# Transposing x and the context by VectorE blocks and a DRAM regroup in place of TensorE, in a self- and cross-attention kernel

## The reference

```python
def _attn(x, ctx, Wq, Wk, Wv, Wo, bo):
    q, k, v = x @ Wq, ctx @ Wk, ctx @ Wv        # 16 heads of 64
    sim = einsum('bihd,bjhd->bhij', q, k) * 64 ** -0.5
    return einsum('bhij,bjhd->bihd', softmax(sim), v) @ Wo + bo
h = _ln(x, g1, be1); x = _attn(h, h, ...) + x
h = _ln(x, g2, be2); x = _attn(h, context, ...) + x
h = _ln(x, g3, be3); y = h @ Wp + bp
x = a * gelu(gate) @ W2 + b2 + x                # a, gate: the halves of y
```

## Time and profile before

| what | value |
|---|---|
| median of 3 runs | 3034.53 us |
| the profiled execution | 3032.93 us, its span 3031.1 us |
| granted TensorE clock over the span | 0.995 |
| PE busy | 2969.6 us (98%) |
| PEld busy | 2591.1 us (85%) |
| DVE busy | 2296.2 us (76%) |
| ACT busy | 1883.4 us (62%) |
| POOL busy | 1424.5 us (47%) |
| DMA traffic | 625.06 MB, mean 206 GB/s |

### The profile page before, as it was taken

The page is one execution under the profiler, slowest core; times in us unless marked ns, Lnnn a source line. Parts: engine busy times, 40 slices in busy tenths (PEclk is TensorE's granted clock), DMA queues, the critical chain, the costliest instruction groups (busy, mean ns, idle before and its releaser), DMA issues. The chain is left out here.

```text
span 3031.1 us, 77419 instructions
## 1 busy us (share of the span) xinstructions
PE 2969.6 (98%) x25600; PEld 2591.1 (85%) x25600; DVE 2296.2 (76%) x3843; ACT 1883.4 (62%) x5618; POOL 1424.5 (47%) x976
## 2 busy tenths in 40 slices
PE   7999999999999999999999999999999979999999
PEld 6888888888888888788888888888888858888888
DVE  6777777777777777788888888888888855566554
ACT  6666666666666667677777777777777633223322
POOL 4555555555555555555555555555555530011000
PEclk9999999999999999999999999999999989999999
DMA  8788888888888888888888888888888830011000
GB/s 240 227 245 244 242 244 248 244 242 245 243 244 244 244 244 239 256 259 255 253 253 254 255 253 252 253 253 253 255 253 252 249 110 28 32 33 33 28 28 21
DMA packets 464444, 625.06 MB, mean 206 GB/s; under 512 B 57745, under 2 KB 397073, under 8 KB 464145
## 3 DMA queue, kind: packets, MB, share of 16 engines
q1 hardware_dynamic: 463024, 624.23, 69.1%
q10 hardware_dynamic: 1376, 0.27, 0.1%
HBM read 330.71 MB, written 293.60 MB: 206 GB/s over the span
## 5 line engine op out<-in xcount | busy, mean ns | idle before, releaser
L586 POOL TENSOR_TENSOR at_probs<-at_probs,at_row_inv 128x1024 f32<-128x1024 f32 x512 | 970.7, 1896 | 1057.8 <-DVE at_row_inv L792 1053.5
L637 ACT ACTIVATE at_probs<-at_ps_s,at_neg_max 128x256 f32<-128x256 f32 x2048 | 948.2, 474 | 143.0 <-DVE at_neg_max L765 94.3
L765 DVE TENSOR_REDUCE at_neg_max<-at_ps_s 128x2 f32<-128x512 f32 x1024 | 660.1, 683 | 193.6 <-PE at_ps_s L943 190.3
L784 DVE STREAM_TRANSPOSE at_blocks<-at_probs 128x1024 f32<-128x1024 f32 x512 | 630.9, 1232 | 2.7 <-POOL at_probs L586 2.0
L690 ACT ACTIVATE at_qk_hi<-at_ps_qk 128x512 fp32r<-128x512 f32 x512 | 305.9, 598 | 322.6 <-PE at_ps_s L943 182.5
L962 PE MATMUL at_ps_o<-at_probs_t,at_v 128*64 128x256 f32 x4096 | 500.3, 386 | 2.0 <-DMA at_probs_t<-at_turns 1.9
L875 PE MATMUL at_ps_qk<-at_h_hi,w_hi 128*128 128x256 f32 x1536 | 431.9, 304 | 11.3 <-ACT at_h_hi L660 4.9
L637 ACT ACTIVATION_READ_ACCUMULATOR at_probs<-at_ps_s,at_neg_max 128x1 f32 x2048 | 416.5, 203 | 0.0
L962 PEld LDWEIGHTS at_ps_o<-at_probs_t,at_v 128*64 128x64 f32 x4096 | 271.8, 137 | 148.9 <-issue 4.0
L875 PE MATMUL at_ps_qk<-at_h_hi,w_lo 128*128 128x256 f32 x1536 | 397.4, 281 | 0.0
L875 PEld LDWEIGHTS at_ps_qk<-at_h_hi,w_hi 128*128 128x128 f32 x1536 | 290.2, 189 | 123.0 <-issue 103.8
(11 more groups left out here) (108 smaller groups left out, 6617.3 us busy)
## 6 DMA issues: line engine op xcount, KB each, us to landing
at_turns<-at_blocks SPq DMA_DIRECT2D x2048, 128.0 KB, 2.5
at_probs_t<-at_turns SPq DMA_DIRECT2D x512, 512.0 KB, 4.4
at_xt<-in_x SPq DMA_DIRECT2D x32, 256.0 KB, 5.4
at_xres<-in_x SPq DMA_DIRECT2D x32, 256.0 KB, 3.3
after_self_attention<-at_yout SPq DMA_DIRECT2D x32, 256.0 KB, 2.6
at_xt<-after_self_attention SPq DMA_DIRECT2D x32, 256.0 KB, 5.6
at_xres<-after_self_attention SPq DMA_DIRECT2D x32, 256.0 KB, 3.6
after_cross_attention<-at_yout SPq DMA_DIRECT2D x32, 256.0 KB, 2.5
```

The source lines that it names most:

```text
L586: pool.tensor_tensor(tile, tile, scale, ALU.mult).then_inc(probs_ready, 1)
L637: last = act.activation(probs[:, slot % 2, h, t], scores[:, slot % 2, h, t], ACT.Exp, bias=neg_max[:, slot % 2, i:i + 1], accum_out=row_su ...
L765: nc.vector.tensor_reduce(neg_max[:, slot, r], scores[:, slot, h], AX_X, ALU.max, negate=True).then_inc(neg_max_ready, 1)
L784: nc.vector.transpose(blocks[:, slot].rearrange("p (j a q) -> p a j q", j=QUADS, q=QUAD), probs[:, slot].rearrange("p h t (k j q) -> p (h ...
```

## The change

For all sequences but the first of the program, the four TensorE transposes of x, the four of the context, and DVE's copy of the context out of the bank go. In their place DVE transposes 32x32 blocks of the normalised x (`turn_x`, at p = 4) and of the context (`turn_context`, at p = 2) into `x_blocks`, one buffer for both; SP stores them in four DMAs of 64 KB each to a DRAM buffer (`store_x`, `store_context`, after the probabilities' stores of that step) and loads them back with one DMA of 256 KB a step later (`load_x_back`, after the probabilities' loads of p = 6; `load_context_back`, after those of p = 4). `scale_shift` moves from step p = 4 to p = 6 on ACT, in front of `high_h`, and reads the loaded buffer `x_back`. The hi part of the context is made by two ACT instructions in place of one, since the source is now in another order. POOL normalises x in place, and one wait for the attention's last stores is added at the start of POOL's feed-forward work.

```diff
             def load_next(b, stage):
-                sp.wait_ge(xnorm_ready, b)
+                if isinstance(b, int) and b == 1:
+                    sp.wait_ge(h_transposed, 1)
+                else:
+                    sp.wait_ge(x_turned, b - 1)
                 sp.dma_start(xt[:], rows(x_in[stage][local])).then_inc(x_loaded, 16)
...
+            def store_bands(buffer, bands, stored):
+                for i in range(QUADS):
+                    sp.dma_start(bands[:, :, i].rearrange("j k n -> k j n"),
+                                 buffer[QUAD * i:QUAD * (i + 1)].rearrange("k (j n) -> k j n", j=QUADS)
+                                 ).then_inc(stored, 16)
+
+            def store_x(b):
+                sp.wait_ge(x_turned, b)
+                store_bands(x_blocks, x_turns, x_turn_stored)
...
+            def load_x_back(b):
+                sp.wait_ge(x_turn_stored, 16 * QUADS * b)
+                sp.dma_start(x_back[:], x_turns.rearrange("j k i n -> (j k) (i n)")).then_inc(x_back_loaded, 16)
...
+                if context and p == TURN_CONTEXT + 2:
+                    load_context_back(b + 1 - n)
+                if ahead(part, stage) and p == TURN_X + 2:
+                    load_x_back(b + 1)
                 for pair in (p, p + 1):
                     if alive(part, pair, TURNED):
                         store_turn(b, pair)
+                if context and p == TURN_CONTEXT:
+                    store_context(b + 1 - n)
+                if ahead(part, stage) and p == TURN_X:
+                    store_x(b + 1)
...
             def scale_shift(b, stage):
-                act.wait_ge(h_transposed, b + 1)
-                if counts(c := b):
-                    act.wait_ge(h_ready, c)
+                first = isinstance(b, int) and b == 0
+                if first:
+                    act.wait_ge(h_transposed, 1)
+                else:
+                    act.wait_ge(x_back_loaded, 16 * b)
+                    act.wait_ge(h_ready, b)
...
             def high_context(b):
-                act.wait_ge(c_t_ready, b - n + 1)
+                act.wait_ge(c_back_loaded, 16 * (b - n + 1))
...
-                act.activation(c_hi[:], c_t[:], ACT.Copy).then_inc(c_hi_ready, 1)
+                for k in range(KT):
+                    last = act.activation(tokens(c_hi[:, k]), by_token(c_t[:])[:, k], ACT.Copy)
+                last.then_inc(c_hi_ready, 1)
...
-                    if ahead(part, stage) and p == TURN_H:
+                    if ahead(part, stage) and p == 6:
                         scale_shift(b + 1, stage_ahead(part, stage))
-                    if ahead(part, stage) and p == 6:
                         high_h(b + 1)
...
-            def context_copy(local):
-                dve.wait_ge(c_transposed, local + 1)
-                nc.vector.tensor_copy(c_t[:].rearrange("p k q -> p (k q)"), ps_misc[:]).then_inc(c_t_ready, 1)
+            def turn_rows(rows, turned_rows):
+                nc.vector.transpose(x_blocks[:].rearrange("p (j a q) -> p a j q", j=QUADS, q=QUAD),
+                                    rows.rearrange("p t (k j q) -> p (t k) j q", j=QUADS, q=QUAD)
+                                    ).then_inc(turned_rows, 1)
...
+            def turn_x(b, stage):
+                dve.wait_ge(xnorm_ready, b + 1)
+                if stage == CROSS:
+                    dve.wait_ge(c_turn_stored, 16 * QUADS * (b - n + 1))
+                elif counts(c := 16 * QUADS * (b - 1)):
+                    dve.wait_ge(x_turn_stored, c)
+                turn_rows(xt[:], x_turned)
...
-                if ahead(part, stage) and p == TURN_CONTEXT and stage_ahead(part, stage) == CROSS:
-                    transpose_context(b + 1)
-                if ahead(part, stage) and p == TURN_H:
-                    transpose_h(b + 1, stage_ahead(part, stage))
```

More of the change, by code:

```diff
@@ L53 @@
 TURN = 2 * TT * TT * QUAD
-TURN_CONTEXT, TURN_H = 2, 4
+TURN_CONTEXT, TURN_X = 2, 4
+X_TURN = TT * KT * QUAD
 V_COLS = INNER // 4
@@ L458, in rows, with by_token, tokens @@
             return seq.rearrange("(t p) d -> p t d", p=P)
+        def by_token(buffer):
+            return buffer.rearrange("p (i t k q) -> p k t i q", i=QUADS, t=TT, k=KT)
+        def tokens(rows):
+            return rows.rearrange("p (t i q) -> p t i q", t=TT, i=QUADS)
         def stored_count(b, q):
@@ L510, in step @@
                         load_turn(b, pair)
+                context = ahead(part, stage) and stage_ahead(part, stage) == CROSS
                 if ahead(part, stage) and p == 0:
                     load_next(b + 1, stage_ahead(part, stage))
+                if context and p == TURN_CONTEXT + 2:
+                    load_context_back(b + 1 - n)
+                if ahead(part, stage) and p == TURN_X + 2:
+                    load_x_back(b + 1)
                 for pair in (p, p + 1):
@@ L642, in scale_shift @@
             def scale_shift(b, stage):
-                act.wait_ge(h_transposed, b + 1)
-                if counts(c := b):
-                    act.wait_ge(h_ready, c)
+                first = isinstance(b, int) and b == 0
[4 more added lines that the diff above has]
+                    act.wait_ge(h_ready, b)
                 for k in range(KT):
-                    last = act.activation(h_t[:, k], ps_misc[:, k * SEQ:(k + 1) * SEQ], ACT.Identity,
+                    out, source = ((h_t[:, k], ps_misc[:, k * SEQ:(k + 1) * SEQ]) if first else
+                                   (tokens(h_t[:, k]), by_token(x_back[:])[:, k]))
+                    last = act.activation(out, source, ACT.Identity,
                                           bias=beta_c[:, stage, k:k + 1],
@@ L814, in step @@
                     turn(b, p + 1)
+                if ahead(part, stage) and p == TURN_CONTEXT and stage_ahead(part, stage) == CROSS:
+                    turn_context(b + 1)
+                if ahead(part, stage) and p == TURN_X:
+                    turn_x(b + 1, stage_ahead(part, stage))
                 if alive(part, p + 1, NORMED):
@@ L881, in project_v @@
                     pe.wait_ge(v_ready, c)
-                if ahead(part, stage) and p == TURN_CONTEXT + 2 and stage_ahead(part, stage) == CROSS:
-                    pe.wait_ge(c_t_ready, b + 2 - n)
-                if ahead(part, stage) and p == TURN_H + 2:
-                    pe.wait_ge(h_t_ready, b + 2)
+                if part == FIRST and p == 0:
+                    pe.wait_ge(h_t_ready, 1)
                 if part in (FIRST, SEAM) and p == 0:
@@ L894, in project_v, with transpose_first @@
                 last.then_inc(v_done, 1)
-            def transposes(src, done):
+            def transpose_first():
+                pe.wait_ge(xnorm_ready, 1)
                 for k in range(KT):
@@ L1005, in _ @@
             pe.wait_ge(ident_made, 2)
[L1006 removed]
+            transpose_first()
             sequences(nc, pe, n, step)
@@ L1112, in _ @@
             pool.wait_ge(f.consts_loaded, 64)
+            pool.wait_ge(before, before_count)
             residual(0, 0)
```

57 lines of the change are left out of this document (30 added, 27 removed).

## The result

The changed kernel took 3133.1 us (median of 4, 3132.5 to 3133.7), the kernel before, beside it on the same chip, 3034.4 us. The ratio is 1.0328, its interval 1.0313 to 1.0343.

A forecast was written before the change was run, and what follows sets the result against it. PE was taken to bound both attention stages. From 3032.9 us, transposes removed gave -42.8, cross-attention stalls +55.7 and self-attention stalls +4.7: 3050.5, stated as 3051 us, range 3004 to 3104 us.

The forecast's parts named there:

- What bounds the kernel: Both attention stages: PE is busy without holes, so work taken off it is saved in full, 0.45 us a batch.
- DVE's turn and SP's stores: Each x and context: DVE's block transpose takes 0.6 us, hidden at p = 4; SP's four stores take 1.9 us.
- The chain behind s: From ACT's scale_shift: lo part of pair 7 ready at s + 3.85, packed lo part of the context at s + 4.91.
- The sum: Cross turn: PE waits for the context's packed lo part, 1.74 us in each of 32 sequences, 55.7 us in all.
- s, the landing of `x_back`: Cross-attention, p = 6: ACT starts scale_shift at s = 1979.4 (1977.8 to 1980.7), with x_back landing in 4.2 us.
- the two cases of the earlier trace: Landing of 256 KB before the change: median 5.5 us behind two 512 KB loads, 3.5 us with none in front.
- My second rival: Much slower: x_back lands in 5.5 us as DMA share rises towards 0.95; cross stall 3.04 us, 3106 us; chance 0.15.
- The probabilities' loads at nothing: Step p = 6: loads go out 1.9 us later but before their use, so cost nothing; at most 1.9 us.
- The stall in self-attention, 4.7 us: Lo part of pair 7 has 0.7 us left; scatter of landings costs 0.15 us for each of 31 sequences (0 to 19).

## Why the prediction was right or wrong

- **What bounds the kernel: right.** PE's time is saved in full wherever nothing else is late: self sequences are 0.45 us shorter, as predicted for a batch.
- **DVE's turn and SP's stores: right.** 0.67 us for 0.6 predicted (`at_x_blocks`, 667 to 671 ns in all 63), 1.83 us for 1.9.
- **The chain behind s: right, but for its last link.** The lo part of pair 7 was ready in time for PE to start at s + 3.78 (predicted s + 3.85); the packed lo part of the context took 0.42 us, as taken. The sum let this packed part decide; at this turn PE did not wait for it (done at 1963.28, read at 1963.63), and the wait for the lo part of pair 7 was the one that counted, 0.25 us less by the prediction's own figures. That PE would wait at the first `project_qk` of a cross sequence, and ACT for `x_back`, was also right.
- **s, the landing of `x_back`: the step that failed, by its size.** Predicted 1979.4; the trace after has 1958.51, which is 1981.3 in the time of the trace before (lining up the scores ahead of the turn, and less the 0.45 us of the transposes). Of the 1.9 us, 1.1 to 1.4 are the landing (5.3 at this turn, 5.6 in the median, against 4.2), and the rest a later issue: the turn stores ahead took 4.59 us, not 3.73. I had put the landing between the two cases of the earlier trace rows as though the loads in front would have drained by 1.6 us; in fact it was that of a transfer behind loads. And I had carried over SP's times of before, though the context's five new DMAs stand ahead on the same queue; x without the context lands in 4.5 us, near the 4.2. PE started 3.3 us late at this turn and 3.1 in the mean, not 1.74: 32 x 1.4 = 45 us of the miss of 82. My second rival had the landing and 3.04 us, with a chance of 0.15; its reason, a DMA share that rises towards 0.95, did not come (0.85 in the stage).
- **The clock: left out.** The sum had no term for it. In the turn shown, a wait of 3.2 us took the clock to 0.50 for 16 matmuls; net 0.7 to 0.95 us a turn, 21 to 30 us. Two experiments show it from both sides, the filled gap and the gap made on purpose.
- **The probabilities' loads at nothing: wrong in size.** PE waits for them for 10.7 us in the cross stage (1.9 before), and for 28.0 us when no other wait covers it. The prediction named this as a thing that would make it wrong.
- **The stall in self-attention, 4.7 us: did not come.** PE is busy 1049.42 of 1050 us. The start, counted at nothing, cost 5.6 us: the `x_back` of sequence 1 landed 5.1 us after its issue at 45.1, ACT waited 2.8 us for it, and PE then 2.6 us at 53.3.

The miss is 3133 - 3051 = 82 us: 45 from the length of the wait, 11 from the probabilities' loads, 30 from the clock, +6 from the start, -5 from the self stall that did not come, and -8 since the three other steps gave back 1.14 us and not 0.90. That leaves 3 us. The wait removed took 108.6 us off (some 8 to 16 of them may come from the values that were left out with it), so that the loss hangs on it is shown; how it splits is worked out from the means of one trace.

## What to carry to other kernels

Work that is taken off the binding engine is worth its whole price only while nothing it replaces comes back later than it did; a round trip through DRAM has to be read by the queue it joins (2.6 us alone, 5.6 us behind two loads), with every new DMA ahead of it counted. Weigh the parts of such a change apart: here two of three gained (3019 us), and the third, whose result came back later than it was wanted, lost more than both. And when a change makes TensorE wait at every turn of a loop, look at its granted clock behind the wait and price that too.

## What the runs showed of the hardware that was not expected

- A gap of 3.1 to 3.2 us on TensorE took its granted clock from 1.00 to 0.50, in the kernel before with idle copies as in the changed one; with a gap of 1.78 us a turn in 4 of 26 was slow, and two gaps of 2.8 and 2.9 us cost nothing of the kind. Of the nominal 1.55 us at the low level only 0.7 to 0.95 were lost in the mean.
- Useless matmuls in such a gap made the kernel 28 us faster.
- A DVE block transpose of a 128x512 f32 tile takes 0.67 us, one of 128x1024 1.23 us. And DVE's subtraction of a 64x256 tile went from 1.03 us to 0.42 us in the median, once POOL's subtraction no longer lay beside it.
